# Mixture of experts in an audio tower: blocks of 384 rows in place of 512, with 70 routed blocks in place of 54

## The reference, cut to what matters

```
h = _L0_tok_ref(x, L0_tok_kernel)
h = h + _L0_attn_ref(_layernorm(h), ...)
h = h + _L0_ffn_ref(_layernorm(h), ...)
h = h + _L1_attn_ref(_layernorm(h), ...)
h = h + _L1_ffn_ref(_layernorm(h), ...)

def _L1_ffn_ref(x, gate_w, gate_b, sw1, sb1, sw2, sb2, rw1, rb1, rw2, rb2):
    t = x.reshape(-1, d)
    hs = gelu(einsum('td,nfd->ntf', t, sw1) + sb1[:, None, :])
    shared = einsum('ntf,ndf->td', hs, sw2) + sb2.sum(axis=0)
    probs = softmax(t @ gate_w.T + gate_b)
    top_v, top_i = top_k(probs, 2)
    cw = zeros_like(probs).at[arange(T)[:, None], top_i].add(top_v)
    hr = gelu(einsum('td,efd->etf', t, rw1) + rb1[:, None, :])
    oe = einsum('etf,edf->etd', hr, rw2) + rb2[:, None, :]
    return shared + einsum('etd,te->td', oe, cw)
```

## Time and profile before

| | us |
|---|---|
| median of 3 executions | 2924.16 |
| lowest and highest of them | 2920.64, 2924.89 |
| the profiled execution: its own time | 2924.89 |
| its span in the profile | 2924.9 |
| `experts`: from the first scatter's stretch to the end (2003.9 to 2924.9) | 921.0 |

### The profile page before, as it was taken

The page is one execution under the profiler, slowest core; times in us unless marked ns, Lnnn a source line. Parts: engine busy times, 40 slices in busy tenths (PEclk is TensorE's granted clock), DMA queues, the critical chain, the costliest instruction groups (busy, mean ns, idle before and its releaser), DMA issues. The chain is left out here.

```text
span 2924.9 us, 52858 instructions
## 1 busy us (share of the span) xinstructions
PE 2456.4 (84%) x16811; PEld 1878.3 (64%) x16811; DVE 2074.9 (71%) x3678; ACT 1665.1 (57%) x3131; POOL 1110.7 (38%) x1340
## 2 busy tenths in 40 slices
PE   7988799999999997559999799973112899999994
PEld 7988454444444445459999799962101788888883
DVE  3555689999999975968888778874000566787875
ACT  3345277777777786335666455451000677777773
POOL 0034022323222233356666333334776000465664
PEclk9999699999999998569999999996555999999997
DMA  3119333333333323611111230002111000577758
GB/s 82 37 46 373 72 57 57 56 56 56 56 58 58 58 33 98 191 28 37 37 38 39 73 137 0 0 1 87 50 50 59 1 1 1 168 246 236 245 177 252
DMA packets 161299, 249.22 MB, mean 85 GB/s; under 512 B 41644, under 2 KB 106901, under 8 KB 154232
## 3 DMA queue, kind: packets, MB, share of 16 engines
q1 hardware_dynamic: 128888, 208.77, 26.3%
q0 software_dynamic: 19712, 38.13, 4.4%
q10 hardware_dynamic: 12544, 0.39, 0.2%
HBM read 155.24 MB, written 93.41 MB: 85 GB/s over the span
## 5 line engine op out<-in xcount | busy, mean ns | idle before, releaser
L1014 ACT ACTIVATE probs<-score 128x748 f32<-128x748 f32 (+1 forms) x768 | 568.4, 794 | 117.5 <-PE score L839 116.2
L943 DVE TENSOR_REDUCE part_max<-to_dve 128x1 f32<-128x512 f32 (+1 forms) x768 | 480.2, 684 | 83.6 <-PE to_dve L820 83.2
L2754 DVE TENSOR_TENSOR m_hid_lo<-m_up,m_hid_hi 128x512 fp32r<-128x512 f32 x408 | 280.4, 688 | 303.2 <-issue 172.3
L820 PE MATMUL to_dve<-k_stack,q_stack 48*128 48x512 f32 (+3 forms) x1536 | 351.5, 367 | 20.1 <-DMA k_stack<-k_parts 19.3
L2650 POOL DMA_INDIRECT e_sums<-m_gated,m_row_in x216 | 212.7, 985 | 389.6 <-DVE m_gated L2772 268.7
L839 PE MATMUL score<-q_stack,k_stack 49*128 49x374 f32 (+1 forms) x1536 | 317.3, 389 | 3.1 <-ACT probs L1014 1.0
L876 PE MATMUL o_sum<-probs,v_sb 128*17 128x374 f32 (+1 forms) x3072 | 315.6, 483 | 0.1
L839 PEld LDWEIGHTS score<-q_stack,k_stack 49*128 49x128 f32 (+1 forms) x1536 | 161.9, 181 | 225.0 <-ACT probs L1014 199.7
L2732 ACT ACTIVATE m_up<-m_up,e_b 128x512 f32<-128x512 f32 x192 | 127.2, 663 | 308.0 <-remote 191.2
L820 PEld LDWEIGHTS to_dve<-k_stack,q_stack 48*128 48x128 f32 (+1 forms) x1536 | 222.9, 187 | 79.3 <-DVE part_max L943 36.6
L2693 PE MATMUL m_down<-m_hid_hi,e_w_hi 128*128 128x512 f32 x192 | 83.3, 434 | 218.5 <-issue 134.9
(11 more groups left out here) (435 smaller groups left out, 6215.3 us busy)
## 6 DMA issues: line engine op xcount, KB each, us to landing
m_weights<-e_records SPq DMA_DIRECT2D x54, 1028.0 KB
q_stack<-q_parts SPq DMA_DIRECT2D x192, 93.5 KB, 3.1
k_stack<-k_parts SPq DMA_DIRECT2D x192, 93.5 KB, 4.1
e_slots<-blank SPq DMA_DIRECT2D x54, 260.0 KB, 3.7
m_row_in<-e_slots SPq DMA_DIRECT2D x54, 260.0 KB
m_weights<-e_sums SPq DMA_DIRECT2D x16, 640.0 KB
e_records<-l_parts SPq DMA_DIRECT2D x16, 512.0 KB, 4.0
v_rows<-v_out SPq DMA_DIRECT2D x16, 408.0 KB, 5.9
```

The costliest lines, as they stand in the source:

```text
L820: last = pe.matmul(ring[i % RING][0:ROWS[c], at_col:at_col + keys.stop - keys.start], q_stack[its_slot][rows, j, c * P:c * P + ROWS[c]], k ...
L943: dve.tensor_reduce(part_max[0:ROWS[c], k, j, c, 0:1], ring[i % RING][0:ROWS[c], :], AX.X, ALU.max).then_inc(used, 1)
L1014: act.activation(probs[0:n, s % 2, m, 2 * j:2 * j + 2, :], score[tile][0:n, :, 0:HALF], ACT.Exp).then_inc(tile_used, 1)
L2754: dve.tensor_tensor(hid_lo[:, f % RING, :], up[f % UPS][:, :], hid_hi[:, f % RING, :].bitcast(F32), ALU.subtract).then_inc(lo_done, 1)
```

## The change

A block and a shared chunk have 384 rows in place of 512, thus 3 tiles in place of 4. By the formula above this gives 70 routed blocks in place of 54. The shared chunks are 32 in place of 24, of which 28 stand in front of the routed blocks in place of 21 (10752 rows in both cases), and 4 behind in place of 3 (1536 rows). The units become 536 in place of 408. The PSUM tiles keep their bank of 512 numbers per partition each, and only 384 are used. The counts of transfers and their sizes follow: a block's rows are 195 KB in place of 260, its weights stay at 1028 KB and are fetched 70 times in place of 54, and the scatters into `e_sums` are 210 in place of 216.

```
-BLOCK = 512
+BLOCK = 384
 SUB = BLOCK // P
 ROUTED = (TOP * B * T + E_N * (BLOCK - 1)) // BLOCK
...
     N = B * TILES
     CHUNKS = N // SUB
-    EARLY = 21
+    EARLY = 28
...
-        turn, back = ps("turn", [P, SUB, P]), ps("back", [P, SUB, P])
-        up = [ps(f"up{k}", [P, BLOCK]) for k in range(UPS)]
-        down = [ps(f"down{k}", [P, BLOCK]) for k in range(2)]
+        turn, back = ps("turn", [P, 4, P]), ps("back", [P, 4, P])
+        up = [ps(f"up{k}", [P, 512]) for k in range(UPS)]
+        down = [ps(f"down{k}", [P, 512]) for k in range(2)]
...
-                        last = pe.matmul(up[f % UPS][:, :], up_weights(m, f - starts[m], part), y[:, m % 2, :],
+                        last = pe.matmul(up[f % UPS][:, 0:BLOCK], up_weights(m, f - starts[m], part), y[:, m % 2, :],
...
-                    act.activation(up[f % UPS][:, :], up[f % UPS][:, :], ACT.Gelu, bias=up_bias(m, f - starts[m])
+                    act.activation(up[f % UPS][:, 0:BLOCK], up[f % UPS][:, 0:BLOCK], ACT.Gelu, bias=up_bias(m, f - starts[m])
```

More of the change, by code:

```diff
@@ L2692, in narrow @@
                     for j, (part, x) in enumerate([(0, hid_hi), (0, hid_lo), (1, hid_hi)]):
-                        last = pe.matmul(down[m % 2][:, :], down_weights(m, f - starts[m], part), x[:, f % RING, :],
+                        last = pe.matmul(down[m % 2][:, 0:BLOCK], down_weights(m, f - starts[m], part), x[:, f % RING, :],
                                          start=(f == starts[m] and j == 0), stop=(f == last_of(m) and j == 2))
@@ L2726, in round_hid @@
                         act.wait_ge(hid_used, f - RING + 1)
-                    act.copy(hid_hi[:, f % RING, :], up[f % UPS][:, :]).then_inc(hi_done, 1)
+                    act.copy(hid_hi[:, f % RING, :], up[f % UPS][:, 0:BLOCK]).then_inc(hi_done, 1)
                 for f in range(ENDS):
@@ L2743, in split_rows @@
                         dve.wait_ge(up_done, starts[m - 1])
-                    flat = turn[:, :, :].rearrange("p q d -> p (q d)")
+                    flat = turn[:, 0:SUB, :].rearrange("p q d -> p (q d)")
                     dve.tensor_copy(y_hi[:, m % 2, :], flat).then_inc(rounded, 1)
@@ L2753, in split_hid @@
                         dve.wait_ge(hid_used, f - RING + 1)
-                    dve.tensor_tensor(hid_lo[:, f % RING, :], up[f % UPS][:, :], hid_hi[:, f % RING, :].bitcast(F32),
+                    dve.tensor_tensor(hid_lo[:, f % RING, :], up[f % UPS][:, 0:BLOCK], hid_hi[:, f % RING, :].bitcast(F32),
                                       ALU.subtract).then_inc(lo_done, 1)
@@ L2760, in keep @@
                         dve.wait_ge(turned_back, m - 1)
-                    dve.tensor_scalar(made[:, m % 2, :], down[m % 2][:, :], down_bias(m), None, ALU.add).then_inc(kept, 1)
+                    dve.tensor_scalar(made[:, m % 2, :], down[m % 2][:, 0:BLOCK], down_bias(m), None, ALU.add).then_inc(kept, 1)
                 def give_back(m):
@@ L2767, in give_back @@
                         h = g.h[:, i * SUB:(i + 1) * SUB, :]
-                        dve.tensor_tensor(h, back[:, :, :], h, ALU.add).then_inc(returned, 1)
+                        dve.tensor_tensor(h, back[:, 0:SUB, :], h, ALU.add).then_inc(returned, 1)
                         return
@@ L2771, in give_back @@
                         dve.wait_ge(sent[(i - 2) % ROWS_IN], 16 * SUB * ((i - 2) // ROWS_IN + 1))
-                    dve.tensor_tensor(gated[:, i % 2, :, :], back[:, :, :],
+                    dve.tensor_tensor(gated[:, i % 2, :, :], back[:, 0:SUB, :],
                                       row_in[:, i % ROWS_IN, :, P + 1:P + 2].broadcast_to([P, SUB, P]), ALU.mult
```

## The result

The changed kernel takes 2953.7 us (median of 4 executions, 2948.7 to 2956.0), the kernel before 2922.4 beside it. The ratio is 1.0107, with a 95% interval of 1.0093 to 1.0122: slower, by about 31 us. The forecast was 2929 with a range of 2919 to 2950; the time lies 4 us over the range's upper end. The profiled execution of the changed kernel took 2954.8 us, with a span of 2952.6, and the two profiles differ by 2952.6 − 2924.9 = 27.7 us.

The account below looks back on a forecast made before the run. PE was taken to bound the shared chunks and routed blocks, transfers the tail, and 2.80 us per PE instruction the stretch beside the scatters. Terms summed to +4.5 us on 2924.9, forecast 2929 us, range 2919 to 2950.

Parts of the forecast that it names:

- Dispatch: Start of the kernel: `passed` and its reduction grow from 432 to 560 numbers, +0.4 us (0 to 0.6).
- The price of a product: PE where saturated: a product of 384 columns takes 0.1754 us, 0.767 of one of 512, about 15 ns being fixed.
- Rival C: PE's products: cost in proportion to columns, no fixed 15 ns, chunks and blocks cheaper, 2917.5 us; chance 0.06.
- Shared chunks: Chunks in front of the routed blocks: 28 of 9.10 us in place of 21 of 11.88, +5.3 us.
- Beside the scatters: Stretch beside the scatters into `e_slots`: length held at 270 us, fewer rows done in it, +5.5 us (0 to +7.7).
- backlog: 2273.8 to 2286.5 us: four waiting units go through ACT and DVE, shorter when narrower, −1.0 us (0 to −1.7).
- Rival A: Scatters' stretch: PE's pace goes by columns, so the +5.5 us falls away, 2924 us; chance 0.12.
- Routed blocks: Routed stage: 70 blocks of 4.93 us in place of 54 of 6.45, PE still the bound, −3.0 us.
- Rival B: Routed stage: bound by supply, PE waiting at L2683 for `weights_in`, blocks of 5.2 us, 2948 us; chance 0.22.
- Last block to its scatter: From the last block to its scatter: 16.35 us become 13.0, blocks having 3/4 of the rows, −3.3 us (0 to −3.9).
- The tail: Last 66.3 us: the same bytes and the same transfers, 0 us (±1.5).
- A pause: Routed stage: one block takes 1.9 us too long; scaled in proportion to the blocks, +0.6 us (0 to 1.9).

Follow-up runs that it names:

- run 1: The changed kernel with four buffers for gated rows in place of two: 2949.7 us, ratio 1.0092 to the kernel before.
- run 2: The changed kernel with eight buffers for incoming rows in place of six: 2952.3 us, ratio 1.0097 to the kernel before.
- run 3: The changed kernel with both four gated buffers and eight row buffers: 2936.6 us, ratio 1.0044 to the kernel before.
- run 9: The changed kernel without weight loads from the fifth block on, later blocks using weights already in their buffers: 2943.2 us, ratio 1.0076 to the kernel before.
- run 10: The kernel before (512 rows) with each scatter into `e_slots` but the first eight held to PE's progress: 2726.3 us, ratio 0.9336.

## Why the prediction was wrong

- **What bounds each stretch: right**, as far as it goes. PE in the shared and routed stages, the transfers in the tail up to its last 5 us, 2.80 us per instruction beside the scatters, which is the pace of PE's reports and not of its work.
- **Dispatch: can't be told.** +0.5 measured for +0.4, in a stretch that differs by 4 to 5 us between profiles of the same width: the agreement is luck.
- **The price of a product: right.** 0.1754 was forecast from products of 374 columns, 0.1763 measured. Rival C (2917.5) is excluded by it.
- **Shared chunks: right in kind, mis-sized.** 9.20 in place of 9.10, thus 28 × 9.195 − 21 × 11.88 = +8.0 for +5.3: 1.2 of the 2.7 are the products, the others the transposes, 0.73 us for 6 and not 0.68.
- **Beside the scatters: the step chose the wrong end.** Two readings were priced, 4.5 us if the fast first part gets through as many rows as before, 7.7 if the same 156 instructions are done, and 5.5 taken. The rows show 156 again. (156 instructions are 317 rows less and not 324, so 7.5 us.) Front less chunks is 15.1 − 8.0 = 7.1, and that is this term with the backlog's (forecast 5.5 − 1.0): 2.6 too low, about as much as two fronts of the same code differ by. PE's gapless stretch came to 24 chunks in 220.7 us, for some 23 in 213. The split into 65 quick instructions and 90 slow ones is too sharp: in the trace of the kernel before, gelus move apart step by step, from 1.3 to 16.8 us over the stretch's first 50 us. Rival A is excluded: gelus stayed 16.80 us apart.
- **Routed blocks: here the prediction failed.** The 4.93 us were right as PE's own pace (4.95). The step "what hides the rest of a block's work" priced DVE, ACT and POOL by how long they work, and not by what they wait for. The wait of `m_gated` for the scatters of two blocks before stands in the code and was left out; so was SP's, for the same scatters, in front of the weights. Issue and landing take 9.8 us at times and 10.8 at the longest, and the change cut the two periods that cover them from 12.9 to 9.9. Runs 1 to 3 and 9 show this wait and its price: 8.7 of the 12.5 us between the −2.4 forecast and the +10.1 measured. Of the other 3.8, 1.4 are PE's own pace (0.02 a block); the rest is not broken down.
- **Rival B**, supply as the bound, came closest in time (2948) and named a wait of PE at L2683 that did come. That is luck: its reason was wrong. With the waits relieved the transfers ran at a share of 0.82 and blocks in 5.00 us (run 3), and a block's transfers came to 4.1 us and not 4.40.
- **Last block to its scatter: right** (−3.2 for −3.3).
- **The tail: wrong by 5 us** that the forecast had no term for, between the last store's landing and the end of the block. They are not in the transfers but in POOL's DRAIN at the program's end, 11.0 us for 3.9; why it is long in some of the programs and not in others stays open.
- **A pause: right** in that there is one; the rule, in proportion to the blocks, was wrong. There is one pause before one gelu, with 70 blocks as with 54; PE lost 1.85 us by it, and 1.8 before.

Together: front +5.3 over the forecast, routed stage +12.5, tail +5.2, the others +0.2: 23.2 us between the forecast's sum of +4.5 and the 27.7 measured.

## What to carry to other kernels

When a block is made smaller, everything that is counted in blocks shrinks in time. Here two buffers came to cover two periods of 9.9 us in place of 12.9, and the slowest landing of a block's last scatter hardly changed (7.0 us before, 6.6 after). So for each wait on a buffer's return, set issue plus landing, the longest and not only the usual one, against the periods that cover it, and look what stands behind the waiting instruction in its queue. And a stretch in which an engine is nearly idle beside another's transfers deserves an experiment before tiles are tuned: there lay 196 us (run 10), against the 31 that the change of width moved.

## What the runs showed of the hardware that had not been expected

- While POOL issued scatters without a break (192 in 251 us), the reports of PE's finished instructions came one per 2.80 us, products of 512 or 384 columns and transposes alike, and up to 68 us late. With the scatters held to PE's progress, one at a time, the same 192 took 279 us at 512 rows (run 10), no report was more than 2.5 us late, and PE lost 35 us in all. The granted clock, 0.53 to 0.56 in the mean of that stretch, is not the reason: 2.80 us are 12 times the 0.2286 us of a product at the full clock. What holds the reports up is not shown by any row, nor whether the profiler's own records have a part in it.
- The last scatter of a block, 128 rows, landed 2.2 us after its start in the median when no weights were loaded (run 9), and 6.0 when loads of 1028 KB went out every 5 us or so (run 2).
- Two waits relieved together took 8.8 us off the routed stage (358.9 to 350.1); the one alone took nothing off (359.1), and the other alone made it longer (369.5).
- ACT stood idle 2.9 to 3.8 us before one and the same gelu in every profile of a width, whatever the transfers did, and PE lost 1.7 to 2.7 us by it.
- POOL's DRAIN at the end of the program took 3.9, 5.2 or 11.0 us; where it took 11.0, 5 us of it stood at the end of the execution with no transfer running.
